# L0 attention's K and V weights of two groups in three tiles, and joint instruction lists around F2 and F3

## What is computed

```
x = x + jnp.tanh(g_xattn[0]) * _L0_xattn_ref(_layernorm(x, axis=-1), ctx_4096, ...)
x = x + jnp.tanh(g_ffn[0]) * _L0_ffn_ref(_layernorm(x, axis=-1), ...)
...
x = x + jnp.tanh(g_xattn[3]) * _L3_xattn_ref(_layernorm(x, axis=-1), ctx_4096, ctx_4096, ...)
x = x + jnp.tanh(g_ffn[3]) * _L3_ffn_ref(_layernorm(x, axis=-1), ...)
```

```
H, KV, HD = (16, 4, 96)
...
hidden = jnp.concatenate([context, latents], axis=1)
...
q = (latents @ Wq.T).reshape(b, q_len, H, HD)
k = (hidden @ Wk.T).reshape(b, s_len, KV, HD)
v = (hidden @ Wv.T).reshape(b, s_len, KV, HD)
...
scores = jnp.einsum('bkgqd,bksd->bkgqs', q, k) * scale
attn = jax.nn.softmax(scores.astype(jnp.float32), axis=-1).astype(q.dtype)
out = jnp.einsum('bkgqs,bksd->bkgqd', attn, v)
...
return out @ Wo.T
```

## Time and profile before

| | us |
|---|---|
| median of 3 runs | 1837.77 |
| lowest, highest | 1837.62, 1842.61 |
| the profiled execution | 1838.21 |
| its span, from first to last instruction | 1836.4 |

### The profile page before, as it was taken

How to read it: one execution, slowest core, us unless ns; L and a number is a source line. 1 busy time by engine, 2 the same in 40 slices (tenths; PEclk the granted TensorE clock), 3 DMA queues, 4 the chain that set the end, 5 groups by cost and what they waited for, 6 DMA issues and landing times. The chain is left out here.

```text
span 1836.4 us, 27639 instructions
## 1 busy us (share of the span) xinstructions
PE 1786.2 (97%) x8872; PEld 1451.0 (79%) x8872; DVE 1240.1 (68%) x2204; ACT 846.4 (46%) x2429; POOL 969.3 (53%) x808
## 2 busy tenths in 40 slices
PE   4999999999999999999999998999999999999998
PEld 3777878777778888888888877878888888888877
DVE  6555655597886666666666678776666666666685
ACT  3465555563544444444345444144544444444451
POOL 2132232255666757566466565274665656756552
PEclk9999999999999999999999998999999999999999
DMA  5010000011101101111011111010110101101001
GB/s 199 8 32 21 24 21 21 24 52 52 58 13 57 35 23 46 29 40 40 17 51 34 35 39 47 12 41 18 51 34 29 46 18 50 40 17 54 20 19 46
DMA packets 37141, 69.47 MB, mean 38 GB/s; under 512 B 4394, under 2 KB 6186, under 8 KB 36946
## 3 DMA queue, kind: packets, MB, share of 16 engines
q1 hardware_dynamic: 37074, 68.61, 12.8%
HBM read 66.50 MB, written 2.10 MB: 37 GB/s over the span
## 5 line engine op out<-in xcount | busy, mean ns | idle before, releaser
L2673 POOL TENSOR_TENSOR probs<-probs,rsums 128x512 f32<-128x512 f32 (+1 forms) x160 | 194.4, 1215 | 312.1 <-DVE rsums L1289 311.6
L2655 POOL TENSOR_TENSOR rope_a<-rope_a,rope_b 128x512 f32<-128x512 f32 x160 | 206.7, 1292 | 161.6 <-DVE rope_b L1264 161.5
L369 PE MATMUL ps<-wo_hiL,ot_hi 128*128 128x512 f32 x608 | 248.6, 409 | 6.9 <-DVE ot_lo L1299 3.7
L369 PE MATMUL ps<-xt_hi,wq_hiL 128*128 128x512 f32 x608 | 241.9, 398 | 0.2 <-DVE xt_lo L1200 0.2
L371 PE MATMUL ps<-wo_hiL,ot_lo 128*128 128x512 f32 x608 | 240.2, 395 | 0.0
L370 PE MATMUL ps<-wo_loL,ot_hi 128*128 128x512 f32 x608 | 240.1, 395 | 0.0
L371 PE MATMUL ps<-xt_hi,wq_loL 128*128 128x512 f32 x608 | 237.8, 391 | 0.0
L370 PE MATMUL ps<-xt_lo,wq_hiL 128*128 128x512 f32 x608 | 236.9, 390 | 0.0
L2078 ACT ACTIVATE probs<-ps,negmax 128x128 f32<-128x128 f32 x512 | 182.1, 372 | 89.4 <-DVE negmax L1271 89.3
L2095 ACT CAST ot_hi<-ps 128x512 fp32r<-128x512 f32 (+1 forms) x160 | 90.7, 567 | 277.9 <-PE ps L371 277.2
L2667 POOL TENSOR_TENSOR q_loL<-rope_a,q_hiL 128x512 fp32r<-128x512 f32 x128 | 164.5, 1295 | 27.4 <-ACT q_hiL L2065 27.4
(11 more groups left out here) (223 smaller groups left out, 4375.3 us busy)
## 6 DMA issues: line engine op xcount, KB each, us to landing
raw<-in_L_proj SPq DMA_DIRECT2D x108, 256.0 KB, 2.7
raw<-in_L_out SPq DMA_DIRECT2D x76, 256.0 KB, 2.6
raw<-in_F_w SPq DMA_DIRECT2D x16, 256.0 KB, 2.8
x<-in_x SPq DMA_DIRECT2D x8, 256.0 KB, 4.0
ct_raw<-in_ctx_t SPq DMA_DIRECT2D x4, 512.0 KB, 7.6
cn_raw<-in_ctx SPq DMA_DIRECT2D x8, 256.0 KB, 9.2
out<-x SPq DMA_DIRECT2D x8, 256.0 KB, 2.0
raw<-in_L_kv SPq DMA_DIRECT2D x8, 192.0 KB, 2.6
```

What stands on the lines that cost most here:

```text
L369: pe.matmul(dst, l_hi, r_hi, start=start, stop=False)
L2655: gp.tensor_tensor(rope_a[:, a], rope_a[:, a], rope_b[:], ALU.add).then_inc(L.s_rsum, 1)
L2673: gp.tensor_tensor(pv, pv, rsums[:, b % 2].unsqueeze(2).to_broadcast([P, GH, L.keys]), ALU.mult).then_inc(L.s_p, 1)
```

## The change

**Weights of L0.** Groups 0 and 1, and groups 2 and 3, share three tiles of 128 columns: [K of the even group | rows 0 to 31 of V of the odd one], [V even | rows 32 to 63], [K odd | rows 64 to 95]. The projections K of the even group, W of the even group and K of the odd one then give, in output rows 96 to 127, a third each of the odd group's V. ScalarE copies these 32 rows apart (into `vw`, four areas that weights or `xn` have elsewhere in time), and the odd group has no W fillers: `FILL_ODD`. The number of weight tiles of L0 falls from 36 to 34, and all counts (`proj_at`, `out_at`, `tile_of`, `last_use`, `bank_user`, `index`) are worked out from one list of all fillers.

**Lists of L0.** `packed_group` becomes `first_group`, `second_group` and `third_group`, each with an order of its own on every engine; the bridge's lists are new, too, for F0, L1, F1 and L2's prologue.

**Lists of L2's end and L3's end.** `last_group` and `feed_forward` go; `middle(a2, a3)` is one list for L2's last group, F2 and L3's prologue, `end(a3)` one for L3's last group and F3. The rows of A3 (the normalised input of L3's attention) are normalised by ScalarE, VectorE computing only the shift (`norm_shift`; before, `norm_rows` on VectorE). New waits: products of batches 0 to 3 of F2 and F3 wait for the last group's transposes, outputs and residuals, turn for the last norm transposes, expert_weight for the last keys_queries.

```diff
+FILL_ODD = {3: [("K", 0), ("Q", 0)], 4: [("Q", 1)], 5: [("V", 0), ("K", 1)], 6: [("Q", 2), ("V", 1)]}
...
-            L.wkv_hi = at(f"wkv_hi{n}", [P, 2, C, hd], F32R, r_wkv)
+            L.wkv_hi = at(f"wkv_hi{n}", [P, 2, C, P], F32R, r_wkv)
...
-        LNS = {"A1": 0, "F1": 8, "A2": 16}
+        LNS = {"A1": 0, "F1": 8, "A2": 16, "A3": 24}
...
-                        rows = P if kind == "Q" else hd
                         for c in range(C):
-                            mm = triple(pe, ps[0:rows, bank, :], w_hi[:, c, :], w_lo[:, c, :],
+                            mm = triple(pe, ps[:, bank, :], w_hi[:, c, :], w_lo[:, c, :],
...
+                def first_group():
...
+                    heads_out(6, 0)
+                    fillers(7, 0, only=1)
+                    out_proj(6, 0)
+                    heads_out(7, 0)
+                    out_proj(7, 0)
+
+                def second_group():
+                    scores(0, 1)
+                    scores(1, 1)
+                    transposes(0, 1)
+                    fillers(0, 1, only=0)
...
+                    transposes(7, 1)
+                    heads_out(6, 1)
+                    out_proj(6, 1)
+                    heads_out(7, 1)
+                    out_proj(7, 1)
+
+                def third_group():
+                    scores(0, 2)
+                    fillers(0, 2, only=0)
+                    scores(1, 2)
+                    transposes(0, 2)
...
+            def middle(a2, a3):
...
+                gates(2, 2)
+                norm_transpose("F2", 4)
+                gates(2, 3)
+                a2.out_proj(7, last)
+                norm_transpose("F2", 5)
+                products(2, 0)
+                norm_transpose("F2", 6)
+                gates(2, 4)
+                products(2, 1)
+                turn(2, 0)
+                products(2, 2)
+                experts(2, 0)
...
+            own = (k[:, :, g], v[:, :, g], k[:, :, g + 1])
+            pairs.append([_np.concatenate([w, v[:, :, g + 1, 32 * n:32 * n + 32]], 2).transpose(1, 0, 2).reshape(P, C * P)
+                          for n, w in enumerate(own)])
```

More of the change, by code:

```diff
@@ L106, in index @@
     def index(self, want, g, b, k, when=NOW):
+        if self.packed:
+            return sum(1 for t in self.order[:self.place(g, b, k, when)] if t[3] in want)
         inside = sum(1 for kind, _ in self.fill[b][:k] if kind in want)
@@ L112, in tile, with bank_user @@
     def tile(self, g, b, k, when=NOW):
+        if self.packed:
+            n = self.place(g, b, k, when)
+            return n, n % 2
         base = self.off[b] + k if when == NOW else self.prologue.index((b, k))
         return (base if when == PROLOGUE else self.per_group * g + base), base % 2
+    def bank_user(self, i, b, k, when):
+        if not self.packed:
+            user = self.two_before(b, k, when)
+            if user is None:
+                return None
+            pb, pk, pw = user
+            kind = self.fill[pb][pk][0]
+            return kind, self.index("KQ" if kind in "KQ" else kind, i, pb, pk, pw)
+        n = self.place(i, b, k, when) - 2
+        if n < 0:
+            return None
+        kind, ahead = self.order[n][3], self.order[:n]
+        if kind == "W":
+            return kind, sum(1 for t in ahead if t[3] == "W" or t[3] == "K" and t[5] % 2)
+        return kind, sum(1 for t in ahead if t[3] in ("KQ" if kind in "KQ" else kind))
     def two_before(self, b, k, when):
@@ L127, in ready @@
     def ready(self, want, g, half):
+        if self.packed:
+            return sum(1 for t in self.order if t[3] in want and
+                       (t[5] < g or t[5] == g and (half == 1 or self.half[t[1]] == 0)))
         if half == 1:
@@ L415, in groups @@
                     if L.packed:
-                        for g in range(L.groups - 1):
-                            group(g, False)
+                        for g in range(L.groups):
+                            packed_group(g)
                     else:
@@ L785, in groups @@
                     if L.packed:
-                        for g in range(L.groups - 1):
-                            packed_group(g)
+                        first_group()
+                        second_group()
+                        third_group()
                     else:
@@ L1009, in bridge @@
                 a0.heads_out(1, last)
+                a0.fillers(2, last, only=1)
+                a0.transposes(2, last)
                 a0.scores(3, last)
-                a0.transposes(2, last)
-                a0.fillers(2, last, only=1)
                 a0.out_proj(1, last)
@@ L1015, in bridge @@
                 a0.scores(4, last)
-                a0.fillers(2, last, only=2)
                 a0.transposes(3, last)
-                a0.out_proj(2, last)
-                a0.heads_out(3, last)
-                a0.scores(5, last)
-                a0.transposes(4, last)
                 pe.wait_ge(Lq[0].s_qk, Lq[0].ready("KQ", last, 1))
@@ L1024, in bridge @@
                 norm_transpose("F0", 0)
+                a0.out_proj(2, last)
+                a0.heads_out(3, last)
+                norm_transpose("F0", 1)
+                a0.scores(5, last)
+                a0.transposes(4, last)
                 a0.out_proj(3, last)
                 a0.heads_out(4, last)
-                norm_transpose("F0", 1)
                 a0.scores(6, last)
@@ L2060, in head @@
                         act.wait_ge(L.s_rsum, m + 1)
-                        src = rope_a[:, a]
+                        src = rope_a[:, L.index("KQ", 0, b, k, when) % 2]
                     else:
                         act.wait_ge(L.s_proj, t + 1)
+                        part = 2 * (P - hd) if odd else 0
+                        piece = act.copy(vw[n, half][part:part + P - hd], ps[hd:P, bank, :])
+                        if odd:
+                            piece.then_inc(L.s_w, 1)
                         src = ps[0:hd, bank, :]
```

2305 lines of the change are left out of this document (1461 added, 844 removed).

## The result

The changed kernel takes **1824.5 us** (median of 5, 1820.97 to 1825.39), the kernel before 1837.77 in the same series: a ratio of 0.992, with an interval of 0.9909 to 0.9931, so 13 us or 0.8% less. The forecast was 1820, in a range of 1805 to 1831.

A forecast was written before the change was run, and what follows sets the result against it. The prediction took TensorE's instruction stream, its idle time and lower-clock stretches as the bound; -22.3 + 13.4 + 5 - 7.3 - 4.3 - 2.4 = -17.9 us against the profiled 1838.21 gave 1820.3, by the median 1820 us, range 1805 to 1831.

The follow-up runs named there:

- l0_early: The change, with the next group's scores 0 and a filler moved ahead of the ends of L0's first and second group, on TensorE, VectorE and ScalarE: 1807.8 us, ratio 0.984.

## What to carry to other kernels

Work that is taken off the bounding engine is worth its time only where it was not the cover of a latency, that is, the time that a result takes to get through the other engines; ask for each removed piece which two steps it stood between, and re-order all the engines' lists together, since a step that is moved on one engine alone waits in the list of the next. Where groups follow each other, let the next one's first step start before the last one's end. And a DMA into a small ring of slots ties together the engine that frees a slot and the one that reads the next tile: a cast that is moved forward by a few places can hold up everything behind it.

## What the runs showed of the hardware

TensorE's clock has two levels here, 2.4 GHz (1.00) and 1.2 GHz (0.50), and the length of an idle time alone didn't tell which one followed. In the change two idle times of 2.85 us between 512-column matmuls had 3.41 us at 0.50 at their end (from 163.08 and from 251.83); the third, which ends at 260.05, had none. The idle time of 3.49 us between score matmuls of 256 columns had 6.83 us at 0.50, which began at 169.91, before it was over (171.60). The second and third group of l0_early stayed at 1.00 with an idle time of 2.31 us in the second. In the last group of the change idle times of 1.05 and 0.49 us close together had a piece of 3.41 us at 0.50 around them, which I had not expected for waits of 1 us; l0_early has the same two waits and no piece there.

The clock also fell with no idle time near. In l0_early the piece from 399.3 in L0's last group comes 15 us after the last idle time (which ended at 383.62); right ahead of it stand 36 matmuls of 72 columns, 0.11 us apart, from 395.05 on. The change has the same matmuls from 414.34 on and no piece behind them. So neither the idle times nor these matmuls by themselves foretell the fall, and what decides it is open.
